# Results of the four-channel slots stored by pairs of channels and quarters of the time, with the 32 batches outermost

## The reference

```
x[64, 128, 2048] float32                            # batch, channel, time
x = x + einsum('bct,bcd->bdt', x, weights[condition])     # one 128x128 matrix of 16 per batch
K[h, l] = 2 Re( sum_n Ct[h, n] * exp(dtA[h, n] * l) )     # 128 channels, 64 modes
y = causal convolution of x with K, along time, per channel; y = y + x * D
out = x + y * (time < length[batch])
```

## Time and profile before

| what | value |
|---|---|
| timed executions | 1277.18, 1277.45, 1262.53 us; median 1277.18 |
| profiled execution | 1265.78 us, of which the span of instructions is 1263.5 us |
| PE / DVE / POOL / ACT busy | 83% / 60% / 49% / 44% of the span |
| granted TensorE clock | 0.934 of full |
| DMA | 330.91 MB, 262 GB/s over the span |
| issues `out<-o_sb` of 256 KB | 254 on SP, 96 of them for wide slots |

### The profile page before, as it was taken

The page is one execution under the profiler, slowest core; times in us unless marked ns, Lnnn a source line. Parts: engine busy times, 40 slices in busy tenths (PEclk is TensorE's granted clock), DMA queues, the critical chain, the costliest instruction groups (busy, mean ns, idle before and its releaser), DMA issues.

```text
span 1263.5 us, 33041 instructions
## 1 busy us (share of the span) xinstructions
PE 1054.1 (83%) x12718; PEld 803.1 (64%) x12718; DVE 756.5 (60%) x1744; ACT 560.3 (44%) x1251; POOL 623.3 (49%) x1396
## 2 busy tenths in 40 slices
PE   8767774777767666785889999999999999999998
PEld 5223342454545444455768888888888878888886
DVE  4989710444334234333567777777777777777775
ACT  3533342333223223323345655655555555555554
POOL 3101427652344442223545757667568558657650
PEclk9988896889878878888999999999999999999999
DMA  9999999999998999998999999999899999999996
GB/s 344 393 340 398 401 353 306 264 307 271 272 264 250 265 246 254 248 245 204 167 209 258 256 210 249 254 227 249 208 272 248 214 260 256 221 249 249 199 243 155
DMA packets 238476, 330.91 MB, mean 262 GB/s; under 512 B 110242, under 2 KB 155682, under 8 KB 230130
## 3 DMA queue, kind: packets, MB, share of 16 engines
q1 hardware_dynamic: 238002, 328.35, 97.9%
q0 software_dynamic: 160, 0.20, 0.2%
q10 hardware_dynamic: 160, 0.26, 0.1%
HBM read 164.96 MB, written 140.71 MB: 242 GB/s over the span
## 4 chain that ended last, share of the span: by engine, by line
PE 53%; DMA 21%; SPq 19%; issue 4%; DVE 2%; ACT 2%; ACTq 0%
PE bank L803 10%; PE bank L822 10%; PE bank L765 8%; DMA u_row<-u_wide 7%; PE bank L747 7%; DMA u_row<-u_full 7%; SPq L435 6%; DMA u_full<-stage 5%; PE bank L781 5%; PE bank L713 5%; PE bank L726 4%; PE bank L809 4%; SPq L385 3%; SPq L387 2%; SPq L449 2%
## 5 line engine op out<-in xcount | busy, mean ns | idle before, releaser
L747 PE MATMUL bank<-ident,u_row 128*128 128x128 f32 x1024 | 287.0, 284 | 138.9 <-DMA u_row<-u_wide 120.2
L803 PE MATMUL bank<-toep,u_t 128*128 128x192 f16 (+1 forms) x3072 | 351.2, 223 | 0.3 <-issue 0.3
L603 POOL TENSOR_TENSOR g_sb<-g_x,g_sb 128x128 f16<-128x128 f32 x256 | 115.3, 484 | 348.5 <-ACT g_sb L891 348.5
L747 PEld LDWEIGHTS bank<-ident,u_row 128*128 128x128 f32 x1024 | 147.1, 145 | 158.9 <-DMA u_row<-u_wide 108.5
L803 PEld LDWEIGHTS bank<-toep,u_t 128*128 128x128 f16 x3072 | 237.0, 100 | 15.3 <-issue 3.9
L1204 DVE SCALAR_TENSOR_TENSOR u_t<-bank,u_t 128x512 f16<-128x512 f32 x256 | 176.3, 689 | 111.1 <-ACT u_t L920 110.0
L809 PE MATMUL bank<-toep,x_t 128*128 128x64 f16 x2048 | 193.2, 195 | 2.0 <-issue 2.0
L822 PE MATMUL bank<-g_sb,st_full 128*128 128x256 f16 x960 | 192.4, 274 | 0.2 <-issue 0.2
L920 ACT ACTIVATE u_t<-bank 128x512 f16<-128x512 f32 x256 | 151.6, 593 | 72.9 <-PE bank L747 72.3
L713 PE MATMUL bank<-x_f,w_buf 128*128 128x512 f32 x280 | 138.0, 644 | 45.6 <-issue 30.7
L765 PE MATMUL bank<-u_t,gt_sb 128*128 128x224 f16 (+1 forms) x1056 | 157.4, 302 | 9.0 <-issue 9.0
(11 more groups left out here) (138 smaller groups left out, 1519.7 us busy)
## 6 DMA issues: line engine op xcount, KB each, us to landing
x_f<-in_x SPq DMA_DIRECT2D x64, 1024.0 KB, 10.5
out<-o_sb SPq DMA_DIRECT2D x254, 256.0 KB
u_full<-stage SPq DMA_DIRECT2D x128, 320.0 KB, 8.9
u_row<-u_full SPq DMA_DIRECT2D x80, 512.0 KB, 6.3
u_wide<-stage SPq DMA_DIRECT2D x128, 192.0 KB, 6.4
u_row<-u_wide SPq DMA_DIRECT2D x96, 256.0 KB, 8.7
toep<-k_scratch SPq DMA_DIRECT2D x88, 256.0 KB, 7.0
g_scratch<-g_sb SPq DMA_DIRECT2D x24, 256.0 KB, 4.5
```

The source lines that it names most:

```text
L747: ins = pe.transpose(bank[:, u_bank(s, q), k % 4 * P:(k % 4 + 1) * P], ap(u_row[b], (h * groups(s) + g) * Q + tb * P, [[1, P]]), ident[:, :])
L803: pe.matmul(bank[:, y, col + tb * P + NM:col + Q], ap(u_t[s % 3], u_at(s, h, tb, a, gr), [[1, P]]), tp[:, hh, b, NM:Q - tb * P], start=fir ...
```

## The change

A wide slot no longer stores each unit with one DMA. It waits for every second unit (v = 1 and v = 3) and then issues four DMAs, one for each quarter t of the time: source the 32 partitions of that quarter with both units (2 x 2 KB a partition), destination with the 32 batches outermost, then the two channels, then 512 elements. So a wide slot stores by 8 DMAs of 128 KB in place of 4 of 256 KB, and the stores of units 0 and 2 stand one `store_out` later. The semaphore counts are adapted (64 for a wide pair, 32 for a full one, summed by `stores_before`). The bytes, the rows of 2 KB and everything on the other engines stay as they were.

```diff
+        def stores_before(s):
+
+            return sum(64 if SLOTS[r].wide else 32 for r in range(s % 2, s, 2) if r < NSL)
...
                 o = 2 * (s % 2) + v // 2
+                if v % 2 == 0:
+                    return
+                sp.wait_ge(s_ov, 4 * s + v + 1)
                 if SLOTS[s].wide:
-                    sp.wait_ge(s_ov, 4 * s + v + 1)
-                    dst = bass.AP(out.tensor, SLOTS[s].part * NBW * H * T + (SLOTS[s].first + v) * T,
-                                  [[UNIT, 4], [H * T, NBW], [1, UNIT]])
-                    sp.dma_start(dst, o_sb[o][:, v % 2, :]).then_inc(s_store[o], 16)
-                elif v % 2 == 1:
-                    sp.wait_ge(s_ov, 4 * s + v + 1)
+                    for t in range(4):
+                        dst = bass.AP(out.tensor, SLOTS[s].part * NBW * H * T + (SLOTS[s].first + v - 1) * T + t * UNIT,
+                                      [[H * T, NBW], [T, 2], [1, UNIT]])
+                        sp.dma_start(dst, o_sb[o][t * NBW:(t + 1) * NBW, :, :]).then_inc(s_store[o], 16)
+                else:
...
-                sp.wait_ge(s_store[o], 32 * (NSL // 2) + 32 * (o == 3))
+                sp.wait_ge(s_store[o], stores_before(NSL + o // 2) + 32 * (o == 3))
...
-                    wait(act, s_store[o], 32 * (s // 2))
+                    wait(act, s_store[o], stores_before(s))
```

## The result

The changed kernel takes 1172.4 us (median of 1171.59, 1172.37, 1172.43 and 1176.26) beside 1274.49 us for the kernel before in the same runs: a ratio of 0.922, with a 95% interval of 0.916 to 0.929. It is faster by 7.8%, some 100 us, where I had forecast 1238 us with a range down to 1208.

A forecast was written before the change was run, and what follows sets the result against it. PE was taken to bound the second half, u_row loads queued behind wide stores the mixing. Savings of 30 + 4 + 0 = 34 us gave 1232 from the profiled 1265.8, 1243 by the median; forecast 1238 us, range 1208 to 1266.

The forecast's parts named there:

- The pieces of 7.62 and 9.55 us: Mixing: landings of a step's fourth u_row load, issued directly behind a wide store, claimed as the chain's longest pieces there.
- part 4: Last stage: four more issues per wide slot, costing up to 13 us or winning at most 7.0; taken as 0.
- Part 2: Moved issues: stores of units 0 and 2 go later in SP's list; nothing counted for it.
- the 7.5 us a step: Mixing: price of a step's four old wide stores, 36.1 us with them less 28.6 without, 1.05 MB at 140 GB/s.
- The first rival: Crowded engines the only bound: new stores add 2.8 us a step, 42 us go in the mixing; 1205 to 1211 us, 15%.
- The step without wide stores: Mixing: the period from step 0's first transpose to step 1's, 28.6 us, taken as the step's price without wide stores.
- The equal queue depths: Mixing: u_full stores landing in 5.3 and 5.1 us at the short period's ends, so 28.6 us isn't borrowed from a filling queue.
- What the new stores add: Mixing: 4.2 us a step, between bytes (3.5 to 2.8) and SP's issues (5.1); step 32.8 us, 30 us saved over nine.
- Part 3: 590.5 to 654.2 us, behind the mixing: 4 us saved, from 0 to 12, with PE idle for 12.4 us.
- Not much faster: New form slow because rows lie 1 MiB apart: gain of 20 us or nothing, middle 10; 1256 to 1262 us, 16%.
- The short step was short for another reason: Step 0 lacks PE's outputs; PE, ACT and SP may keep most of 7.5 us: 9 us gained, 1257 to 1262 us, 12%.
- SP becomes the bound: SP pays for every new issue: 22 us more in the mixing, 13 in the last stage; 1301 us, 7%.

The follow-up runs named there:

- moved4: Changed kernel with the old form of store (one DMA a channel, 4 quarters outermost) at the new places: 1271.6 us, ratio 1.000 to the kernel before.
- nowide: Changed kernel without any store of a wide slot, their results left out of the output: 1140.6 us, ratio 0.898 to the kernel before.
- New_last: Changed kernel with the old store for the first twelve wide slots, the new one for the twelve of the last stage: 1246.3 us, ratio 0.978.
- row16: Changed kernel's four issues of 128 KB, each partition written as one 4 KB row, 16 batches outermost, then 2: 1179.8 us, ratio 0.929 to the kernel before.
- new_first: Changed kernel with the new stores for the first twelve wide slots only, the old store in the last stage: 1196.9 us, ratio 0.939.
- One_channel: Changed kernel with only the first channel of each pair stored, 4 issues of 64 KB: 1165.6 us, ratio 0.917 to the kernel before.
- row8: Changed kernel's four issues of 128 KB, each partition written as one 4 KB row, 8 batches outermost, then 4: 1187.5 us, ratio 0.934.
- spread16: Changed kernel with pairs stored by single channels, 8 DMAs of 64 KB in a row, 16 batches outermost, then 2: 1299.8 us, ratio 1.020.

## Why the prediction was wrong

**What bounds each stage** was read rightly in the mixing: PE waits for loads of `u_row` that queue behind wide stores. One detail was not. The pieces of 7.62 and 9.55 us are not the longest of the chain. The longest stands behind a store whose issue was not stretched; the chain has both:

```profile
387.67 0.55 SPq L449
388.26 11.12 DMA u_row<-u_wide
```

So the length of the issue in front does not tell how late a load will land. In the last stage PE is the main bound, but not the only one, see part 4. Part 2 (the moved places are worth nothing) is confirmed by moved4.

**The forecast's mechanism** was the right one: the old stores were dear by their form, and a form with a larger outermost count takes the price away. What failed is a size. The step of the prediction that went wrong is the 7.5 us a step that the old stores were said to cost, where leaving them out shows 10.3. The first rival, in which the crowded engines are the only bound, is nearer to what happened, but even that rival stopped at 1205 us, since it used the same 7.5. The terms that were mis-sized, against 94 us in the two traces, with 34 in the sum:

*The step without wide stores.* I took one period, from step 0 to step 1, 28.6 us, for the price of everything else. It is one sample, and of another kind than the mean that I took it from. The same period is 28.0 us in nowide, but the nine that follow there, still without a wide store, are 25.8 on the mean: 27.7 for the four with three batches, less for the others. So of the 2.8 us between 28.6 and 25.8 some 1.9 come from setting a step of three batches beside steps of 2.7 on the mean, and 0.9 from the single sample. The equal queue depths answer neither. With 25.8 the old stores are worth 10.3 us a step and not 7.5. This is 2.8 x 9 = 25 us of the 60 that are missing.

*What the new stores add.* I added 4.2 us to the step, the middle between bytes (2.8 to 3.5) and SP's issues (5.1). Measured are 3.2 us on top of 25.8. The upper end, SP's issues at full price, was wrong: I had argued that a list without gaps must grow by each issue put into it. But the old four issues already took 5.4 us of SP a step, stretched, and the new eight take 5.8, and the loads of `u_row` behind them are issued faster, too. A list without gaps isn't a busy one. What the 3.2 us are made of stays open. 1 us x 9 = 9 us.

*Part 3*, the four steps behind the mixing: 17 us where I took 4, above my bound of 12. I had bounded the gain by PE's idle time (12.4 us), which did fall, to 4.3 us. The rest is a matter of the cut: it is made at SP's place in the program, and SP is further ahead of PE at its end now, so that 642 of PE's matmuls lie in the stretch and not 758, and 95 more lie in the last stage. Missing: 13 us.

*Part 4*, the last stage: 14 us where I took 0 and bounded the gain by PE's 7.0 us of waits for `u_row<-u_full`. New_last shows that the wide stores do lie on PE's path there. PE's idle time in this stage fell from 28 to 13 us. The waits for `u_row`, 7 us, are gone, but the pauses that the view puts down to "issue" were more, 16.0 us in six rows, and are 7.8 us now. The largest of them, the input matmuls of the states, before and after:

```profile
PE bank L765 <- issue: 7.7, 6, 2.0
```

```profile
PE bank L771 <- issue: 0.8, 2, 0.4
```

I had bounded the gain by the waits that name a load and left out those that name nothing. With the 95 matmuls that moved into it, this stage gains some 6 us more than its length shows (95 x 65 ns), and part 3 as much less.

**The rivals.** *Not much faster* by the addresses (16%): refuted by row16 and the changed kernel, whose rows lie 1 MiB apart, too; with them the nine steps move 300 and 312 GB/s in place of 254. The table of row pitches that I cited (the Trainium skill, "DMA: Bandwidth & Descriptors", section "Latency and other measured facts") gives an estimate of 5.1 to 6.4 us for a slot's stores. Measured are 3.2 us on top of the step without them, so it did not decide here. *The short step was short for another reason* (12%): no. With the wide stores left out and PE back at its outputs (nowide), the steps are shorter still, 25.8 us. *SP becomes the bound* (7%): not with 8 issues a slot; with 16 the kernels were slower than the kernel before (1.012 to 1.020).

**The chances.** Faster than 2% had 0.67 and was right, but the range ended at 1208 us because its lower side was worked out from the same 28.6 us as the forecast; a bound that rests on the same sample as the middle is no bound.

**What stays open.** Why the step does not come below 29 us with the new stores, when half the bytes bring only 0.8 of the 3.2 us that leaving them out brings; how much of them SP's issues are and how much the bytes; and what the last stage gains exactly, 14 us in the traces and 20 to 32 in the medians.

## What to carry to other kernels

Look at the outermost count of each side of every DMA: four stores of 256 KB with 4 outermost cost 10.3 us a step, some 100 GB/s, eight of 128 KB with 32 outermost cost 3.2 us, and the loads queued behind them landed in 4.8 in place of 8.7 us. When you price something by a period that lacks it, first count what else the two periods hold: here three batches stood against 2.7 on the mean, and one period against nine. And an issuing queue without gaps whose issues have very unequal lengths (537 to 4873 ns) is partly waiting: eight issues took 5.8 us of a step where four had taken 5.4, but sixteen took 12.0 and became the bound.

## What the runs showed of the hardware that was not expected

The length of a DMA's issue on SP went with the form and not with the bytes. Median issue of the wide store: 438 ns for 32 partitions to 32 x 2 x 512 (128 KB), 428 ns to 32 x 512 (64 KB), but 592 ns when the 32 batches are split into 16 x 2 (both at 64 KB and 128 KB), 661 to 666 ns for 8 x 4, and 598 ns for one DMA of 512 KB. Such a median still depends on how full the queues are: the form of the changed kernel has 528 ns in new_first, where all its issues lie in the mixing and just behind it, and 431 ns in new_last, where all lie in the last stage. One_channel, row16 and row8 (the row of the changed kernel stands above):

```profile
L456 SPq DMA_DIRECT2D out<-o_sb x192: 336/428/2074, 277.1 to 1121.0; - x192
```

```profile
L456 SPq DMA_DIRECT2D out<-o_sb x192: 557/593/2292, 275.5 to 1140.2; - x192
```

```profile
L456 SPq DMA_DIRECT2D out<-o_sb x192: 661/666/3182, 278.7 to 1153.3; - x192
```

So the changed kernel's issues are cheaper than the 590 ns that I had priced, and spread16's, at 592 ns, are not. The granted clock of PE in the mixing steps rose with its busy share, 0.84 to 0.92 with the new stores and 0.96 without any, so part of what better loads bring comes back a second time as faster matmuls (PE is busy for 214 us in place of 229, with 2172 matmuls on record in place of 2157).
